# A four-stage attention chain on one core: block transposes on VectorE, kept flags and norm rows as rows, folded copies, a new order

## The chip, the cores and the metric

One core of a Trainium2 chip. The metric is the device time of the whole kernel in microseconds. In the text PE is TensorE, ACT is ScalarE, DVE is VectorE, POOL is GpSimd and SP is SyncE, whose queue issues the DMAs.

## The reference

The input is x and a context, both 128 batches x 128 tokens x 256 channels, f32, and a third array of 64 channels. Four layers run one after the other on every batch:

```python
# L0, 16 heads of 16
mask0 = 1 - all(x == 0, axis=2)
x1 = layernorm(x + mha(x, x, mask0, causal=True))
x2 = layernorm(x1 + mha(x1, context, mask1))     # mask1 from x1
x  = layernorm(x2 + (relu(x2 @ fc1.T + b) * mask0 @ fc2.T + b) * mask0)
# L1, queries x, keys and values norm(context)
nf, nx = norm(x), norm(context)
cross = gelu(attention(nf, nx, nx) @ fc1.T + b) @ fc2.T + b    # width 4 inside
nc = norm(cross)
x = nf + gamma2 * (cross + gamma1 * attention(nc, nc, nc))
# L2
x = x + softmax(x @ context.T) @ context
# L3, 8 heads of 32, then a scan over the 128 tokens
x = x + mha(norm(x), norm(context))
s[t] = silu(s[t-1] @ A.T) + u[t]                 # u from norm(x), 64 states
return x + s @ C + mod
```

In L0, a head's number of valid keys is the count of nonzero energies in its first row, and the masks multiply Q, K, V and the output. The mask on the context's keys and values is the one of x1's tokens.

## The kernel before

**Groups and lags.** Batches go in 64 groups of two. Each engine has a list of steps written out by hand of the form unit.step@lag (PROGRAM, from line 139), and `drive` (line 252) runs 64 + 6 iterations: in iteration i a step with lag l works on group i - l. So at any time groups of seven ages are in work, and a period is one pass through an engine's list. Every step waits on semaphores for what it reads and for its buffer, and engines work strictly in the order of their lists. PSUM has eight banks; which one a step takes is fixed in BANKS. After the 70 iterations all engines meet, and the scan over tokens runs for all 128 batches at once (from line 1582).

**Units.** self_in, self_att, ctx_in, ctx_att and ffn are L0; pair is L1; real is L2; mix_in, mix_att and mix_out are L3. The data of a group stands either "natural" (tokens in partitions; tiles `nat`) or turned (channels in partitions; tiles `trn`, in the profile "turned"), and PE turns the one into the other: a step of four 128x128 transposes against the identity (`turn4`, line 553, line 557 in the profile) into one PSUM bank, which ACT copies out (`evac`, line 903, line 912 in the profile). The steps of this kind that matter here are self_in.xT (x), ctx_in.cT (the context times the flags of x1), real.ccT (the context), and pair.CT (the context normalised, `nat["HC"]`). The context's tile `nat["CC"]` is loaded once more for the last two. A turned x feeds the projections q, k, v (line 565 and 573); the context likewise; the turned normalised context feeds the keys and values of L3 and, scaled by weights (NXT, line 1271), the keys of L1.

**Small work.** POOL multiplies the context by the kept flags (mask, line 1513), copies the flags on so that later groups can overwrite them (lines 1471 to 1484), and adds and scales the norms. The values of L0 leave PSUM by ACT (into VN) and are multiplied by the valid flags on DVE (vp, line 1243). The number of valid keys takes nz, count and spread on DVE, then a matmul by ones (len). The softmaxes of L1 and L2 take a maximum, then a multiplication by minus the scale (nm, line 1288). ACT keeps a copy of x1 for the residual (x1r, line 959).

**The end.** The scan's fresh input and residual lie in DRAM. Its SBUF tile for the input is the upper half of `shared`, where also keys, weights and loaded x tiles of the pipeline live. SP issues the first big piece in iteration 68, inside load_mod of group 62 (scan_early, line 515), after a list of waits for what still uses that memory; it then stores the residual of group 62, behind it in the same queue. res (line 1334), the step of DVE that overwrites the stored tile, waits for that store.

Of the kernel before, what the change touches and what calls it, by code (L numbers as in the profile page):

```python
# [110 lines left out]
def latest(*counts):  # L111

    high = {}
    for c in counts:
# [26 lines left out]
        mix_att.scores.00@6 pair.cross@5 ctx_att.turn.11@4 ctx_att.turn.12@4 ctx_att.values.01@4  # L141
        ctx_att.values.03@4 ctx_att.values.02@4 ctx_att.values.00@4 ctx_att.turn.13@4 ctx_att.turn.10@4
        mix_in.k@5 ctx_att.values.11@4 ctx_att.values.10@4 ctx_att.values.12@4 ctx_att.values.13@4
        ctx_att.back.0@4 real.ccT@5 ctx_in.x1T@3 ctx_att.back.1@4 self_att.scores.00@2 self_att.scores.01@2
        self_att.scores.02@2 mix_att.turn.02@6 ctx_in.cT@3 pair.ncT@5 ctx_in.q@3 pair.sc2@5 mix_att.turn.03@6
        ctx_in.k@3 pair.pT2@5 self_att.scores.11@2 self_att.scores.03@2 self_att.scores.10@2 mix_att.turn.00@6
        pair.av@5 self_in.len@2 self_att.turn.01@2 mix_att.turn.01@6 ffn.x2T@4 mix_att.values.03@6
        mix_att.values.02@6 ctx_in.e0@3 mix_att.values.00@6 mix_att.values.01@6 self_in.xT@1 ffn.fc1@4
        self_att.turn.00@2 self_att.turn.02@2 real.x4T@5 ffn.fc2@4 real.screal@5 mix_out.o@6 self_att.turn.03@2
        real.pTreal@5 self_att.scores.12@2 self_att.scores.13@2 ctx_att.scores.01@3 self_att.values.01@2  # L150
        self_att.values.02@2 self_att.values.00@2 self_att.values.03@2 self_att.turn.11@2 real.av@5 self_in.k@1
        self_in.q@1 self_att.turn.13@2 ctx_in.len@3 self_att.turn.10@2 mix_out.h6T@6 ctx_in.v@3
        self_att.back.0@2 ctx_att.scores.03@3 ctx_att.scores.02@3 ctx_att.scores.11@3 ctx_att.scores.00@3
        self_att.turn.12@2 self_in.v@1 pair.CT@4 self_att.values.13@2 self_att.values.10@2 self_att.values.11@2
        self_att.values.12@2 ctx_att.scores.13@3 ctx_att.scores.12@3 real.h5T@5 ctx_att.turn.01@3 pair.FT@4
        mix_in.v@4 pair.sc1@4 self_att.back.1@2 ctx_att.turn.00@3 mix_in.q@5 ctx_att.turn.02@3 ctx_att.turn.03@3
        pair.pT1@4 self_in.e0@1 pair.av1@4 mix_out.u@6 ctx_att.scores.10@3
    """,
    "act": """
        self_att.probT.13@3 self_att.probT.10@3 self_in.q@2 ctx_in.v@4 pair.lnC@5 pair.lnF@5 self_att.probT.12@3  # L160
        real.ln5@6 self_in.v@2 pair.HCT@5 ctx_att.exp.01@4 self_att.outT.1@3 ctx_att.exp.00@4 ctx_att.exp.03@4
        real.h5T@6 pair.FT@5 ctx_att.probT.01@4 ctx_att.exp.02@4 ctx_att.exp.11@4 mix_in.v@5 ctx_att.probT.00@4
        pair.exp1@5 ctx_att.exp.12@4 mix_in.q@6 ctx_att.probT.02@4 pair.pT1@5 ctx_att.probT.03@4 pair.gelu@5
        self_att.ln1@3 pair.cross@5 ctx_att.exp.13@4 ctx_att.exp.10@4 ctx_att.probT.12@4 mix_att.exp.02@6
        ctx_att.probT.11@4 ctx_att.probT.10@4 ctx_att.probT.13@4 ctx_att.outT.0@4 pair.lnN@5 ctx_att.outT.1@4
# [37 lines left out]
        mix_out.mod@6 ffn.biased@3 self_in.keys@1 self_att.add@2  # L203
# [62 lines left out]
def build(nc, dram):  # L266
# [6 lines left out]
    with ExitStack() as ctx:  # L273
# [25 lines left out]
        for _ in range(16):  # L299
            next(part)  # L300
# [151 lines left out]
        with nc.Block() as block:  # L452
# [637 lines left out]
            def _(dve):  # L1090
                def norm_steps(key, unit, src, ready):
# [3 lines left out]
                    def stats_(g):  # L1095
                        for w in latest(*ready(g)):
                            dve.wait_ge(*w)
# [640 lines left out]
```

## Time and profile before

| | us |
|---|---|
| median of 2 runs | 4029.62 |
| lowest and highest | 4024.6, 4034.65 |
| the profiled execution's own time | 4030.49 |
| its span | 4028.7 |
| PE, ACT, DVE, POOL busy | 3835.5, 3502.7, 3405.5, 2895.3 |

The span is from the first to the last instruction of the profiled execution; its own time is what the device reports for it. Busy times are over the whole span. A number like L557 is a line of the kernel; where a helper records every operation, all its users have that line and are told apart by the names of their tiles.

### The profile page before, as it was taken

How to read it: one execution, taken by the hardware profiler on the slowest of the kernel's cores; microseconds unless marked ns; L12 is line 12 of the kernel's file. 1: busy time of each engine (PE TensorE's matmuls, PEld its weight loads, DVE VectorE, ACT ScalarE, POOL GpSimd, SP SyncE). 2: the span in 40 equal slices, each digit the busy share in tenths (PEclk: the TensorE clock that was granted, in tenths of full speed). 3: DMA queues.
4: the chain of work that ended last, by engine and by line, in shares of the span. 5: the costliest groups of instructions: out<-in, count | busy, mean ns of one | idle time of the engine just before them, and what ended most of it. 6: DMA issues, size and time to landing. Idle time of an engine off the chain costs nothing. (4 is left out here: it accounts for less than half of the span.)

```text
span 4028.7 us, 111616 instructions
## 1 busy us (share of the span) xinstructions
PE 3835.5 (95%) x37177; PEld 3207.8 (80%) x37177; DVE 3405.5 (85%) x9519; ACT 3502.7 (87%) x8460; POOL 2895.3 (72%) x3172
## 2 busy tenths in 40 slices
PE   5999999999999999999999999999999999999859
PEld 3788888888888888888888888888888888888637
DVE  3788988888888898888888898888888898888635
ACT  2899999999999999999999999999999999999735
POOL 1577777777777777777777777777777777777635
PEclk7999999999999999999999999999999999999979
DMA  3001011001101100110111011011101100110038
GB/s 114 20 30 34 19 34 34 26 26 34 34 21 32 34 28 24 34 34 21 32 34 31 21 34 34 23 30 35 34 19 34 34 28 24 34 34 24 16 93 303
DMA packets 121875, 159.92 MB, mean 40 GB/s; under 512 B 12296, under 2 KB 108450, under 8 KB 116642
## 3 DMA queue, kind: packets, MB, share of 16 engines
q1 hardware_dynamic: 116896, 145.39, 11.7%
q8 instruction: 306, 5.01, 0.5%
q10 hardware_dynamic: 4416, 7.41, 0.5%
q14 instruction: 257, 2.11, 0.2%
HBM read 114.86 MB, written 37.75 MB: 38 GB/s over the span
## 5 line engine op out<-in xcount | busy, mean ns | idle before, releaser
L621 PE MATMUL bank<-ident,prob 128*128 128x128 f32 x5120 | 757.1, 280 | 62.6 <-ACT CR L1008 24.5
L941 ACT ACTIVATE probT<-bank 128x512 f32<-128x512 f32 x1280 | 733.4, 596 | 93.9 <-PE bank L621 92.5
L621 PEld LDWEIGHTS bank<-ident,prob 128*128 128x128 f32 x5120 | 572.8, 142 | 233.9 <-issue 138.3
L930 ACT ACTIVATE prob<-prob,mx 128x128 f32<-128x128 f32 x2048 | 646.5, 399 | 23.2 <-DVE mx L1130 23.0
L912 ACT ACTIVATE turned<-bank 128x512 f32<-128x512 f32 x896 | 524.5, 603 | 141.0 <-PE bank L557 109.1
L565 PE MATMUL bank<-turned,shared 128*128 128x256 f32 x2560 | 598.8, 381 | 0.7 <-ACT turned L912 0.7
L1447 POOL TENSOR_TENSOR rs_ln<-ve_ln,half 128x2 f32<-128x2 f32 x320 | 251.2, 785 | 444.8 <-DVE ve_ln L1112 444.8
L1141 DVE TENSOR_REDUCE mx<-bank 128x4 f32<-128x512 f32 x768 | 508.9, 684 | 40.7 <-PE bank L592 38.1
L565 PEld LDWEIGHTS bank<-turned,shared 128*128 128x128 f32 x2560 | 474.0, 191 | 59.0 <-ACT turned L912 1.1
L1152 DVE TENSOR_TENSOR prob<-bank,mx 128x512 f32<-128x512 f32 x768 | 509.5, 677 | 6.7
L922 ACT ACTIVATE prob<-prob 128x512 f32<-128x512 f32 x768 | 461.2, 641 | 10.0 <-DVE prob L1152 9.1
L1526 POOL TENSOR_SCALAR shared<-turned,half_of 128x512 f32<-128x512 f32 x256 | 400.9, 1580 | 87.3 <-ACT turned L912 87.3
L592 PE MATMUL bank<-shared,turned 32*128 32x256 f32 x4096 | 447.5, 403 | 2.3 <-ACT probT L941 1.4
L1123 DVE TENSOR_TENSOR prob<-bank,causal 128x512 f32<-128x512 f32 x512 | 350.3, 684 | 85.7 <-PE bank L621 78.0
L1130 DVE TENSOR_REDUCE mx<-prob 128x4 f32<-128x512 f32 x512 | 348.5, 681 | 22.2 <-ACT prob L930 1.8
L573 PE MATMUL bank<-shared,turned 128*128 128x256 f32 x1536 | 365.4, 381 | 0.4 <-DVE turned L1259 0.2
L592 PEld LDWEIGHTS bank<-shared,turned 32*128 32x128 f32 x4096 | 283.4, 185 | 80.1 <-issue 67.3
L573 PEld LDWEIGHTS bank<-shared,turned 128*128 128x128 f32 x1536 | 278.1, 191 | 31.2 <-DVE turned L1259 1.1
L1461 POOL TENSOR_TENSOR X<-X,row_ln_g 128x512 f32<-128x512 f32 x192 | 244.9, 1276 | 75.3 <-ACT X L991 75.3
L1537 POOL TENSOR_TENSOR prob<-prob,inv 128x512 f32<-128x512 f32 x256 | 266.5, 1042 | 28.8 <-DVE inv L1168 28.7
L655 PE MATMUL bank<-probT,shared 128*32 128x128 f32 x8192 | 277.8, 276 | 0.6 <-ACT probT L941 0.6
L655 PEld LDWEIGHTS bank<-probT,shared 128*32 128x32 f32 x8192 | 208.4, 110 | 65.6 <-issue 43.8
(238 smaller groups left out, 9058.9 us busy)
## 6 DMA issues: line engine op xcount, KB each, us to landing
shared<-in_x SPq DMA_DIRECT2D x128, 256.0 KB, 2.8
CB<-in_ctx SPq DMA_DIRECT2D x64, 256.0 KB, 4.0
CC<-in_ctx SPq DMA_DIRECT2D x64, 256.0 KB, 2.7
mod<-mod_rows SPq DMA_DIRECT2D x64, 256.0 KB, 3.7
residual<-X SPq DMA_DIRECT2D x64, 256.0 KB, 2.2
out<-turned SPq DMA_DIRECT2D x16, 1024.0 KB, 5.0
turned<-residual SPq DMA_DIRECT2D x14, 1024.0 KB, 7.8
u_turned<-us SPq DMA_DIRECT2D x124, 32.0 KB, 1.9
```

Source lines behind the costliest of these rows:

```text
L565: last = nc.tensor.matmul(t[:, m * W:(m + 1) * W], w[:, a, m * 128:(m + 1) * 128], src[:, a, :], start=(a == 0), stop=(a == DH - 1))
L573: last = nc.tensor.matmul(t[:, b * D:(b + 1) * D], src[:, a, b * S:(b + 1) * S], w[:, a, :], start=(a == 0), stop=(a == DH - 1))
L592: last = nc.tensor.matmul(t[:, a * W:(a + 1) * W], QT[p][rows_, a, b * S:(b + 1) * S], KEYS[p][rows_, a, :, b * S:(b + 1) * S], start=True ...
L621: last = nc.tensor.transpose(t[:, h * 128:(h + 1) * 128], src[:, h, :], ident[:])
L655: last = nc.tensor.matmul(t[k * 32:(k + 1) * 32, r * 128:(r + 1) * 128], VP[p][:, b, 4 * r + k, :], src[:, k, :], start=True, stop=True)
L912: nc.scalar.activation(dst, banks.of(f"{unit}.{name}")[:, 0:n], ACT.Copy).then_inc(*st["act"].mark(name))
L922: nc.scalar.activation(flat(t), flat(t), ACT.Exp, scale=SCALE[p]).then_inc(*st["act"].mark(f"exp.{b}{r}"))
L930: last = nc.scalar.activation(t[:, h, :], t[:, h, :], ACT.Exp, bias=low[:, h:h + 1], scale=1.0)
L941: nc.scalar.activation(flat(t), banks.of(f"{att}.turn.{b}{r}")[:, :], ACT.Copy).then_inc(*st["act"].mark(f"probT.{b}{r}"))
L1141: nc.vector.tensor_reduce(m[:], banks.of(f"{att}.tile.{b}{r}")[:, :].rearrange("p (h t) -> p h t", h=4), AX, ALU.max)\
L1152: nc.vector.tensor_tensor(t[:], banks.of(f"{att}.tile.{b}{r}")[:, :].rearrange("p (h t) -> p h t", h=4), maxes.of(f"{att}.max.{b}{r}")[:]. ...
L1526: last = nc.gpsimd.tensor_scalar(KEYS[p][:, :, c, :], KT[p][:], half_of[:, c:c + 1], None, ALU.mult)
```

## The change

1. **x and the context arrive in blocks.** Instead of one DMA per group with rows of 1 KB, four DMAs place blocks of 32 tokens x 32 channels such that one DVE transpose of 128x512 (32x32 blocks) gives the turned tile. self_in.xT moves from PE and ACT to DVE; ctx_in.cT too, now of the unmasked context, into one of three buffers ccT. The plain x is still loaded (XR); its flags are now taken from that.
2. **The kept flags as a row.** ctx_in.kept on PE turns the flags, each broadcast over 128 columns (two transposes), and ctx_in.masked on DVE multiplies ccT by them from PSUM. POOL's mask goes.
3. **real.ccT goes**: real.screal reads the same ccT. The context's plain tile becomes one of three buffers cc in the memory of `shared`; its load moves from lag 3 to lag 2 and waits for real.av three groups back.
4. **Norm rows through DRAM.** lnC's scale and shift (two per token) are stored to DRAM (rowout) and loaded as rows, broadcast to all partitions (rowin). POOL makes the turned normalised context from ccT by a multiplication and an addition (pair.hcs, pair.HCT). lnC and HCT on ACT and CT on PE go; NXT reads SBUF.
5. **Folded.** nz takes its sum along (count goes), spread goes into the len matmul; valid writes its flags straight to where vp needs them; v of both passes leaves PSUM by vp on DVE; the maximum of L1 and L2 is negated in place (nm goes), the scale moves into the weights' scaling or into an evacuation; four copies of flags and x1r go, by more buffers.
6. **New PROGRAM and BANKS** for all engines. The highest lag stays 6.
7. **scan_early waits for more**, because ccT and cc lie where the scan's input goes.

```diff
+    def in_blocks(t, src, g, here):
+        v = t[:].rearrange("p b d -> p (b d)").rearrange("p (a b k i) -> p a b k i", a=DH, b=G, i=32)
+        for j in range(4):
+            sp.dma_start(v[32 * j:32 * j + 32], src[g, j]).then_inc(here.sem, 16)
...
     def load_pair(g):
-        for w in latest(real["pe"].before("av", g)):
+        sp.wait_ge(added, 7)
+        for w in latest(ctx_in3.before(g), real["pe"].before("av", g, 3)):
             sp.wait_ge(*w)
-        sp.dma_start(nat["CC"][:], ctx_g[g]).then_inc(ctx_in3.sem, 16)
+        sp.dma_start(cc[g % 3], ctx_g[g]).then_inc(ctx_in3.sem, 16)
...
     def scan_early():
         n = NG - 1
-        for w in latest(self_in["pe"].done("xT", n), self_in["dve"].done("amax", n), self_in["pool"].done("keys", n),
+        for w in latest(self_in["dve"].done("xT", n), self_in["dve"].done("amax", n), self_in["pool"].done("keys", n),
+                        self_in["pe"].done("v", n), ctx_in["dve"].done("masked", n), pair["pool"].done("HCT", n),
+                        real["pe"].done("screal", n), real["pe"].done("av", n),
...
+    def kept(g):
...
+        for b in range(G):
+            last = nc.tensor.transpose(t[:, b * S:(b + 1) * S], keep1[g % 4][:, b:b + 1].to_broadcast([128, 128]), ident[:])
...
+    def x_turned(g):
+        waits_apart(dve, prep, *latest(x_in.done(g), *(self_in["pe"].before(n, g) for n in "qkv")))
+        nc.vector.transpose(flat(trn["XT"]), x_blocks.rearrange("p b d -> p (b d)")).then_inc(*self_in["dve"].mark("xT"))
...
+    def mask(g):
...
+        nc.vector.tensor_tensor(trn["CBT"][:], ccT[g % 3], t[:, 0:W].unsqueeze(1).to_broadcast([128, DH, W]), ALU.mult)
...
-        nc.vector.tensor_scalar(nz[p][:], banks.of(f"{unit}.e0")[:, 0:S], 0.0, None, ALU.not_equal)
+        nc.vector.tensor_scalar(nz[p][:], banks.of(f"{unit}.e0")[:, 0:S], 0.0, 0.0, ALU.not_equal, ALU.add, accum_out=counts[p][:])
...
+    def hcs(g):
...
+        nc.gpsimd.tensor_tensor(trn["HCT"][:], ccT[g % 3], norm_row[:, 0, :].unsqueeze(1).to_broadcast([128, DH, W]), ALU.mult)
...
     "sp": """
-        self_in.load@0 mix_out.load@6 ctx_in.load@2 mix_out.store@6 self_att.load@2 mix_out.store_u@6
-        pair.load@3
+        mix_out.load@6 pair.rowin@4 pair.load@2 self_in.load@0 ctx_in.load@2 mix_out.store@6 mix_out.store_u@6
+        self_att.load@1 pair.rowout@3
     """
```

In PE's list the context's value steps stood as 01 03 02 00 and, behind two turns and mix_in.k, 11 10 12 13; they now stand as 01 00 02, then 03 12 11, then 13 10, with turns between. real.av is the 64th of the 96 steps of PE's new list (99 before), ctx_in.cT the 13th of the 110 of DVE's.

## Rows read from the trace of the kernel before

In a timeline a row is start (us), length (us), engine, line, operation, tiles and count. In groups a row is busy time in all (us), mean of one (ns), then idle time of the engine before it. By source, durations are least/median/greatest.

**Rows 1.** The page's first part: the span, and each engine's busy time.
```profile
span 4028.7 us, 111616 instructions
...
PE 3835.5 (95%) x37177; PEld 3207.8 (80%) x37177; DVE 3405.5 (85%) x9519; ACT 3502.7 (87%) x8460; POOL 2895.3 (72%) x3172
```

**Rows 2.** Windows, ten periods of the steady part: us, then busy time of each engine.
```profile
1000.00:1585.30 585.30, 574.10 (x5642) 484.11 (x5641) 520.43 (x1461) 536.50 (x1281) 442.20 (x490) 1.00 0.10 30
```

**Rows 3.** The gelu's instructions (line 1001) between 1000 and 3400 us, first and last start.
```profile
L1001 ACT ACTIVATE y5T<-bank,gate_col x82: 359/360/362, 1053.2 to 3394.8; 4x128 f32<-4x128 f32 x82
```

**Rows 4.** Waits from 200 to 3690 us: in total, times, longest (us).
```profile
PE bank L621 <- ACT CR L1008: 23.8, 60, 0.5
...
PE bank L621 <- ACT prob L922: 21.6, 59, 0.4
...
PE bank L761 <- ACT probT L941: 19.3, 55, 0.4
```

**Rows 5.** Timeline of PE in one steady period: start us, us, what.
```profile
1706.03 0.60 PE L557 MATMUL bank<-ident,CC 128*128 128x128 f32 x4
1706.46 0.60 PE L557 MATMUL bank<-ident,X 128*128 128x128 f32 x4
...
1720.16 0.66 PE L557 MATMUL bank<-ident,shared 128*128 128x128 f32 x4
1720.66 1.89 PE L565 MATMUL bank<-turned,shared 128*128 128x256 f32 x8
...
1742.65 0.60 PE L557 MATMUL bank<-ident,HC 128*128 128x128 f32 x4
1743.18 1.08 PE L655 MATMUL bank<-probT,shared 128*32 128x128 f32 x32
1744.19 1.14 PE L592 MATMUL bank<-shared,turned 32*128 32x256 f32 x8
```

**Rows 6.** Groups of instructions, shapes apart: busy us, mean ns, then idle before them.
```profile
L991 ACT ACTIVATE HC<-CC,nmr_lnC,rs_lnC 128x256 f32<-128x256 f32 x128 | 71.3, 623 | 0.8 <-POOL nmr_lnC L1452 0.8
```

**Rows 7.** DVE: groups by line, then two lines that run once, by source.
```profile
L1152 DVE TENSOR_TENSOR prob<-bank,mx 128x512 f32<-128x512 f32 x768 | 509.5, 677 | 6.7
...
L1275 DVE TENSOR_SCALAR turned<-bank,col_n_w,col_n_b 128x256 f32<-128x256 f32 x128 | 63.7, 539 | 8.6 <-ACT turned L968 3.7
...
L1249 DVE COPY shared<-valid_self 128x32 f32<-128x32 f32 x64 | 36.7, 574 | 0.0
...
L1291 DVE TENSOR_SCALAR nmax<-nmx 128x2 f32<-128x2 f32 x128 | 17.7, 138 | 0.1
...
L1360 DVE TENSOR_TENSOR shared<-shared,turned x1: 2283/2283/2283, 46.4 to 46.4; 128x2048 f32<-128x2048 f32 x1
...
L1386 DVE TENSOR_SCALAR w_q<-w_q,col_g x2: 342/343/344, 57.1 to 58.1; 128x256 f32<-128x256 f32 x2
```

**Rows 8.** The page's DMA parts: the main queue, and the residual store.
```profile
q1 hardware_dynamic: 116896, 145.39, 11.7%
...
residual<-X SPq DMA_DIRECT2D x64, 256.0 KB, 2.2
```

**Rows 9.** Timeline of SP's queue near the end of the pipeline.
```profile
3853.28 0.46 SPq L448 DMA_DIRECT2D shared<-u_turned  x1
3853.79 0.86 SPq L450 DMA_DIRECT2D turned<-residual  x2
3889.60 0.41 SPq L509 DMA_DIRECT2D residual<-X  x1
```

**Rows 10.** Windows while the residual chunks load: last columns are clock, DMA share, GB/s.
```profile
3873.00:3913.00 40.00, 21.87 (x138) 16.09 (x138) 13.00 (x35) 11.65 (x24) 11.18 (x13) 0.74 0.17 64
```

**Rows 11.** By source, at the end: real.av; what res (line 1337) waited for; the store's landing.
```profile
L784 PE MATMUL bank<-CC,pct_real x4: 379/379/454, 3883.6 to 3884.3; 128*128 128x256 f32 x4
...
  DMA residual<-X: 7.8, 1
...
DMA to landing us min/median/max: 24.4/24.4/24.4
```

More of the change, by code:

```diff
@@ L140 @@
     "pe": """
[L141 to L155, printed above, removed]
@@ new lines @@
+        pair.rs2@5 self_att.max.00@2 self_att.mask.03@2 pair.sa@5 self_att.max.03@2 self_att.mask.02@2
+        self_att.max.02@2 self_att.mask.10@2 ctx_in.nz@3 self_att.mask.11@2 ffn.relu@4 self_in.vp@2
+        self_att.max.10@2 self_att.max.11@2 self_in.xT@1 ffn.sum@4 ctx_in.valid@3 ffn.ln3stats@4 ffn.ln3aggr@4
+        ffn.ln3ve@4 real.mxreal@5 self_in.amax@2 pair.lnCve@3 mix_out.res@6 real.rsreal@5 mix_out.ln6stats@6
+        self_att.mask.13@2 self_att.mask.12@2 mix_out.ln6aggr@6 self_att.max.13@2 ctx_att.max.01@3
@@ new lines @@
+        self_att.max.12@2 ctx_att.centre.01@3 mix_out.ln6ve@6 real.x5@5 pair.lnFstats@4 pair.lnFaggr@4
+        pair.lnFve@4 real.ln5stats@5 self_in.keep@2 real.ln5aggr@5 real.ln5ve@5 ctx_att.max.00@3
+        self_att.recip.0@2 ctx_att.max.02@3 ctx_att.centre.00@3 self_att.norm.0@2 ctx_att.max.03@3
+        ctx_att.centre.02@3 ctx_att.centre.03@3 ctx_in.vp@3 ctx_att.max.11@3 self_att.recip.1@2 self_in.q0@1
+        pair.NXT@4 self_att.norm.1@2 ctx_att.max.12@3 ctx_att.centre.11@3 pair.mx1@4 ctx_att.centre.12@3
@@ new lines @@
+    mix_in.k:2 ctx_att.out.1:3 ctx_in.x1T:1 ctx_att.back.0:4 mix_att.turn.02:7 ctx_att.back.1:2
+    self_att.tile.00:2 self_att.tile.02:0 self_att.tile.01:6 pair.ncT:4 ctx_in.q:3 pair.sc2:0 mix_att.turn.03:1
+    ctx_in.kept:5 ctx_in.k:3 pair.pT2:1 mix_att.turn.00:4 self_att.tile.10:6 self_att.tile.11:7
+    self_att.tile.03:5 pair.av:1 mix_att.turn.01:2 self_att.turn.01:4 ffn.x2T:3 mix_att.out.0:5 ctx_in.e0:2
+    ffn.fc1:0 self_att.turn.02:4 self_att.turn.00:1 real.x4T:4 ffn.fc2:7 self_in.len:7 self_in.v:3 real.screal:1
@@ new lines @@
+    mix_out.o:7 self_att.turn.03:2 self_att.turn.11:2 real.pTreal:0 ctx_att.tile.01:3 self_att.tile.13:5
+    self_att.tile.12:6 self_att.out.0:4 real.av:0 self_in.k:7 self_att.back.0:0 self_in.q:6 self_att.turn.12:3
+    self_att.turn.10:1 mix_out.h6T:3 self_att.turn.13:7 ctx_att.tile.00:1 ctx_att.tile.03:4 ctx_att.tile.02:5
+    ctx_in.len:0 ctx_in.v:2 self_att.out.1:7 ctx_att.tile.11:6 ctx_att.tile.13:1 ctx_att.tile.12:3 real.h5T:0
+    pair.FT:4 ctx_att.turn.01:5 mix_in.v0:2 mix_in.v1:0 pair.sc1:7 self_att.back.1:7 ctx_att.turn.00:4
@@ L226 @@
+    mix_in.q:5 ctx_att.turn.02:7 ctx_att.turn.03:2 pair.pT1:4 self_in.e0:6 mix_out.u:4 pair.av1:5
 """.split())
```

398 lines of the change are left out of this document (189 added, 209 removed).

## Prediction

> **What bounds the kernel now.** I read the page first. PE is busy for 3835.5 of the 4028.7 us span, ACT for 3502.7 and DVE for 3405.5 [rows 1]; but these are means over a filling, a steady part, a draining and the scan. So I took a stretch of the steady part by windows: in 585.3 us PE is busy 574.1, ACT 536.5, DVE 520.4, POOL 442.2, at a granted clock of 1.00 [rows 2]. The gelu of ScalarE runs once per group of two batches, so its start times give the period: two instructions each, 41 pairs from 1053.2 to 3394.8 us, 2341.6/40 = 58.54 us [rows 3]. Ten periods are that stretch, so per period PE has 57.4 us, ACT 53.7, DVE 52.0 and POOL 44.2. PE is the bound. Of its 1.1 us of idle time nearly all is a wait for ScalarE: 23.8 + 21.6 + 19.3 us in the 59.6 periods from 200 to 3690 us [rows 4]. What counts is therefore what a period costs on PE, times some 61 periods that run at this pace, and then what happens at the ends, which the period does not show.
>
> **PE, per period.** The timeline shows four transposes starting at 1706.03 and the next step at 1706.46: 0.43 us for a group of four (real.ccT; ctx_in.cT has the same 0.43). self_in.xT takes 0.50 until the projection behind it starts and pair.CT 0.53 [rows 5]. All four go: 0.43 + 0.43 + 0.50 + 0.53 = 1.89. ctx_in.kept adds two transposes of the same shape, half a group: 0.22. The new order also splits the eight value steps of the context pass, which now run as two groups of four, in three; one run of four takes 1.01 us to the next start [rows 5], and I put 0.1 for the extra opening and closing (bounds: nothing, and 0.4, another such run less its work). Net 1.57 saved. Scores still come in six runs of different row groups, so they stay.
>
> **ACT.** Nine instructions go, of about 0.62 each: the evacuations of xT, cT, CT, ccT and both v, the X1r copy, and the two halves of the lnC normalisation [rows 6]: 5.5 us, so ACT falls from 53.7 to 48.1. It is under PE now and stays there, so this pays only through the 1.1 us that PE waits for it. I take a third of that back, 0.35; bounds 0 and 1.1. The new period is then 58.54 - 1.57 - 0.35 = 56.6.
>
> **DVE.** Removed: two counts, two spreads and three negations of 0.14 to 0.3, two copies into a stride (0.57 the dearer), and the two NXT halves read SBUF instead of PSUM, 0.54 down to the 0.34 of a scaling of the same size [rows 7]: together 2.7 us of durations, and seven waits of DVE for itself. Added: two block transposes of 128x512, and a masking multiplication from PSUM (the 0.68 of the centring). The trace has no DVE transpose. Nearest row: 0.68, any pass over 128x512. Upper bound: the 2.28 us of a pass over four times as many elements, as if a 4-byte element took four turns [rows 7]; lower bound 0.3, half of the nearest row (a transpose can't give time back). I take 0.7, which gives +2.1 against -2.7, and up to 0.3 for the sum that now rides on the nz comparison: DVE stays at 51.5 to 52, under 56.6, hidden behind PE. At 2.28 each it would be 54.8.
>
> The Trainium skill (VectorE: DVE Perf Modes, The three transpose paths) gives 311 ns for a DVE transpose of 128x128 bf16 in 32x32 blocks and says such a transpose stays inside its blocks, which is why the loads have to place the blocks. Four such would be 1.24 us by an estimate from that page; DVE would have 53 us and the forecast would stand. No run here shows it yet.
>
> **POOL** loses two masking passes and four tiny copies, and gains two passes over 128x512 for the norm of context: about level, 44 of 56.6.
>
> **DMA.** x and one of the context loads become four DMAs each with runs of 32 floats, 2 x 2048 descriptors of 128 bytes per period, 256 per DMA engine. The main queue's 116896 packets took 11.7% of 16 engines' span, 64 ns each at a mean of 1.2 KB [rows 8]; if 128 bytes cost as much, that is 16 us of the 57, and I expect less. The SP queue now puts the context load of a group behind real.av of the same iteration (pair.load waits for it), and behind it come self_in.load and ctx_in.load. real.av is the 64th of PE's 96 steps, and ctx_in.cT the 13th of DVE's 110 in the next iteration, so by their places about (0.33 + 0.12) x 56.6 = 25 us are left for up to 16. The norm rows leave at the end of one iteration and are wanted in the middle of the next. I put nothing.
>
> The skill speaks against this part (DMA: Bandwidth & Descriptors, Specifications): below 512 bytes the engines lose line rate. By that the loads are slow, but it changes the sum only if they exceed the 25 us, which is a rival below.
>
> **The end, where I expect a loss.** At iteration 68 SP issues scan_early: 3.9 MB of fresh scan input at 3853.28 and then two residual chunks at 3853.79 [rows 9]. Those have 122 batches as partitions. The store of residual (62), issued at 3889.60 in the same queue, takes 24.4 us to land, where 2.2 is the median, because it lies behind them, and res(63) on DVE waits 7.8 us for it [rows 8, 9, 11]. While the chunks run, DMA is busy at 0.17 only [rows 10]: about two of the sixteen engines, and the whole takes from 3853.3 to 3914.0, 61 us. The change adds waits to scan_early, because cc and ccT now lie in the scan's memory: real.screal and real.av of group 63. real.av(63) starts its matmuls at 3883.6 and ends about 3884.7 [rows 11]. So scan_early leaves 31 us later, everything behind it too, and res(63), which has no cover left (it is waiting already), goes from 3914.0 to about 3945. The scan follows it by the same steps as now. Price 31 us; bounds 0 (if something else reorders) and 38. Queued behind the waiting SP are the stores of (62), whose landing has its own delay, already counted.
>
> **Sum.** 61 x 1.92 = 117; the three shrinking iterations before the end save about 3 more; the end costs 31: 89 less. The profiled execution's own time is 4030.49 (1.8 us around the span); 4030.5 - 89 = 3941.5, and the median of the two runs is 0.9 below it. I give 3942, 2.2% less. 2% is 81 us, about what a measurement of this kernel can tell from no change.
>
> **Rivals.**
> 1. PE's remaining waits go altogether (ACT relieved by 5.5 us): period 55.9, 4030.5 - 61 x 2.64 - 3 + 31 = 3898. For it: nearly all PE idle is ScalarE's. Against it: DVE is now the second bound, at 92%. Chance 0.13.
> 2. The end doesn't lengthen: 3911. Against it stand the added waits. Chance 0.10.
> 3. The waits stay or new ones come, because evacuation moved from ACT (idle 4.9 us) to DVE, whose work doesn't shrink while the period does: period 57.0 to 58.2, 3965 to 4038, middle 3990. Chance 0.24.
> 4. The other side: the block transposes are slow and DVE becomes the bound. At 2.28 us each DVE has 54.8 us of work, and it now stands idle for 6.5 us a period; if 5 of these stay as latency the period is 59.8 and the time 4030.5 + 61 x 1.26 + 31 = 4138. It decides from about 1.6 us per transpose (53.5 + 5 = 58.5). Chance 0.05.
> 5. The changed loads don't arrive in the 25 us: each us that cT is late is a us of period; only above 64 ns x 1.5 per packet. Or the loads aren't split as written. 4060 to 4100. Chance 0.03.
> The forecast case has the remaining 0.45, with 3915 to 3972 as its own span.
>
> **How the numbers follow.** Faster by over 2% (below 3949): 0.27 of the forecast case, all of 1 and 2: 0.50, and 0.02 of 3: 0.52. Slower by over 2% (above 4110): half of 4 and 5 with a little of unknown kinds: 0.05. The rest, 0.43, within 2%. Range 3893 to 4022: it leaves out 4 and 5, the upper end of 3 and the lower of 1.
>
> **What would show it.** Right: gelu starts 56.6 us apart; PE about 55.8 busy per period, ACT 48, DVE about 52; four-transpose groups of X (shared), CB, CC and HC gone; a DVE transpose near 0.7 us; the scan input issued right after real.av(63), and res(63) waiting some 39 us for the residual's DMA. Wrong: a period over 57.2 with PE idle, DVE above 54, long waits of DVE transposes for DMA, or scan input that leaves before real.av(63).

## The result and the profile after

The changed kernel takes 3986.64 us (median of two runs, 3986.45 and 3986.82) against 4029.62: a ratio of 0.9893, 95% interval 0.9877 to 0.9909. It is 1.1% faster. I had forecast 2.2%, 3942 us, so about half of the forecast gain came, and the time stands inside my range and in the band of my third rival.

The first lines of the page, which answer to [rows 1] and [rows 8]:

```profile
span 3985.0 us, 108660 instructions
...
PE 3772.9 (95%) x36281; PEld 3090.5 (78%) x36281; DVE 3380.8 (85%) x9264; ACT 3267.6 (82%) x7884; POOL 2860.4 (72%) x2916
...
DMA packets 401412, 176.68 MB, mean 44 GB/s; under 512 B 316425, under 2 KB 379811, under 8 KB 396195
...
q1 hardware_dynamic: 396448, 162.33, 18.5%
```

PE has lost 62.6 us, ACT 235, and the main queue moves 3.4 times as many packets.

The steady part first. The gelus, now line 1012, answer to [rows 3]:

```profile
L1012 ACT ACTIVATE y5T<-bank,gate_col x84: 357/358/361, 1041.5 to 3391.6; 4x128 f32<-4x128 f32 x84
```

41 periods in 2350.1 us: 57.32 us each, where I had said 56.6. But they are not alike. Windows over three single periods, to be laid beside [rows 2] (us, busy time of PE, PEld, DVE, ACT, POOL, granted clock, DMA share, GB/s):

```profile
1442.29:1499.35 57.06, 56.44 (x552) 46.59 (x551) 51.57 (x143) 50.03 (x120) 43.73 (x46) 1.00 0.16 36
1499.35:1556.40 57.05, 56.43 (x552) 46.51 (x551) 51.35 (x143) 50.03 (x120) 43.49 (x45) 1.00 0.16 35
2070.94:2131.90 60.96, 58.02 (x556) 47.86 (x552) 51.89 (x144) 50.14 (x120) 44.09 (x48) 0.97 0.22 33
```

The undisturbed period is 57.05 us. The third took 60.96 with the same work. Of the 57 periods from the fourth gelu to the 61st, 13 are more than 0.3 us above the median, and all 57 together are 17.6 us above it; in the kernel before the same sum was 1.0 us. How much it is differs from execution to execution: two kernels below with the same stores (blocks_plain, tail_split) have 31.3 and 33.2 us in their profiles. Where the span changed, by the gelus' starts (us):

```
                         before    after   difference
start to 4th gelu         350.7    350.3     -0.4
4th to 61st (57 periods) 3336.5   3269.6    -66.9   (-83.4 by the median period, +16.6 irregular, rest rounding)
61st to 64th              164.2    159.4     -4.8
64th to first scan step    75.8    104.4    +28.6
scan                      101.5    101.3     -0.2
```

The end was as expected. SP's timeline (start, length), to be compared with [rows 9], and under it, by source, what res (L1342) waited for, beside [rows 11]:

```profile
3810.16 0.48 SPq L449 DMA_DIRECT2D shared<-u_turned  x1
3810.69 0.86 SPq L451 DMA_DIRECT2D turned<-residual  x2
3814.98 29.88 SPq L527 DMA_DIRECT2D residual<-X  x1
3844.90 7.09 SPq L559 DMA_DIRECT2D shared<-us  x2
...
  DMA residual<-X: 38.7, 1
```

The store of residual (62) needs 29.9 us only to be issued, and res(63) stands 38.7 us (I had said some 39).

Groups of DVE and POOL (busy us, mean ns, then idle before them):

```profile
L1261 DVE TENSOR_TENSOR shared<-bank,shared 128x512 f32<-128x512 f32 x128 | 87.8, 686 | 59.2 <-PE bank L593 59.2
...
L1203 DVE STREAM_TRANSPOSE turned<-shared 128x512 f32<-128x512 f32 x64 | 44.9, 701 | 4.7 <-DMA shared<-in_x 4.7
L1209 DVE STREAM_TRANSPOSE shared<-CB 128x512 f32<-128x512 f32 x64 | 44.8, 700 | 0.0
...
L1509 POOL TENSOR_TENSOR turned<-shared 128x512 f32<-128x512 f32 x64 | 83.6, 1306 | 0.0
```

The block transposes take 0.70 us as estimated. The block loads keep them waiting 4.7 us in the whole run, all of it at one time.

### The profile page after: what moved, and what is told of

The parts are those of the page before. It is cut to its first block and busy times, and to the rows that moved or that the text cites. A ratio compares the mean times of both kernels' runs of the same rounds, so it can differ in the third digit from the quotient of the medians.

```text
span 3985.0 us, 108660 instructions
## 1 busy us (share of the span) xinstructions
PE 3772.9 (95%) x36281; PEld 3090.5 (78%) x36281; DVE 3380.8 (85%) x9264; ACT 3267.6 (82%) x7884; POOL 2860.4 (72%) x2916
## 5 line engine op out<-in xcount | busy, mean ns | idle before, releaser
L641 PE MATMUL bank<-ident,prob 128*128 128x128 f32 x5120 | 767.9, 279 | 13.5 <-DVE mx L1147 5.3
L641 PEld LDWEIGHTS bank<-ident,prob 128*128 128x128 f32 x5120 | 585.2, 142 | 162.4 <-issue 97.5
L585 PE MATMUL bank<-turned,shared 128*128 128x256 f32 x2560 | 617.0, 384 | 19.8 <-DVE turned L1203 19.5
L932 ACT ACTIVATE turned<-bank 128x512 f32<-128x512 f32 x704 | 410.3, 592 | 198.5 <-PE bank L577 179.1
L942 ACT ACTIVATE prob<-prob 128x512 f32<-128x512 f32 x768 | 471.9, 631 | 6.4 <-DVE prob L1158 5.4
L1453 POOL TENSOR_TENSOR rs_ln<-ve_ln,half 128x2 f32<-128x2 f32 x320 | 223.9, 700 | 333.5 <-DVE ve_ln L1118 333.5
L675 PE MATMUL bank<-probT,shared 128*32 128x128 f32 x8192 | 316.0, 278 | 32.7 <-ACT probT L961 25.2
L1129 DVE TENSOR_TENSOR prob<-bank,causal 128x512 f32<-128x512 f32 x512 | 341.3, 677 | 2.9 <-PE bank L612 2.0
L675 PEld LDWEIGHTS bank<-probT,shared 128*32 128x32 f32 x8192 | 198.3, 109 | 139.7 <-issue 77.1
L1468 POOL TENSOR_TENSOR X<-X,row_ln_g 128x512 f32<-128x512 f32 x160 | 204.0, 1275 | 96.8 <-ACT X L1002 94.9
```

Source lines behind the costliest of these rows:

```text
L585: last = nc.tensor.matmul(t[:, m * W:(m + 1) * W], w[:, a, m * 128:(m + 1) * 128], src[:, a, :], start=(a == 0), stop=(a == DH - 1))
L641: last = nc.tensor.transpose(t[:, h * 128:(h + 1) * 128], src[:, h, :], ident[:])
L675: last = nc.tensor.matmul(t[k * 32:(k + 1) * 32, r * 128:(r + 1) * 128], VP[p][:, b, 4 * r + k, :], src[:, k, :], start=True, stop=True)
L932: nc.scalar.activation(dst, banks.of(f"{unit}.{name}")[:, 0:n], ACT.Copy, scale=scale).then_inc(*st["act"].mark(name))
L942: nc.scalar.activation(flat(t), flat(t), ACT.Exp, scale=SCALE[p]).then_inc(*st["act"].mark(f"exp.{b}{r}"))
```

## What an irregular period looks like

ACT's timeline in the period that took 60.96 (in brackets the idle time before, and what ended it), then PE's:

```profile
2079.73 0.65 ACT L942 ACTIVATE prob<-prob 128x512 f32<-128x512 f32 x1
2082.81 0.60 ACT L976 ACTIVATE outT<-bank 128x512 f32<-128x512 f32 x1 [2.43 <-remote]
2083.30 0.59 ACT L932 ACTIVATE turned<-bank 128x512 f32<-128x512 f32 x1
...
2087.91 1.08 ACT L932 ACTIVATE turned<-bank 128x512 f32<-128x512 f32 x2 [3.01 <-PE bank L577]
```

```profile
2079.42 0.43 PE L675 MATMUL bank<-probT,shared 128*32 128x128 f32 x8 [0.29 <-ACT probT L961]
...
2080.71 0.38 PE L768 MATMUL bank<-ident,keep 128*128 128x128 f32 x2
2083.55 1.08 PE L688 MATMUL bank<-ident,outT 128*128 128x128 f32 x4 [2.46 <-ACT outT L976]
2084.43 2.94 PE L585 MATMUL bank<-turned,shared 128*128 128x256 f32 x8
```

ACT stops for 2.43 us and the profile finds no releaser in the core ("remote"). What it waits to copy has long been computed (PE's value steps, L675, end at 2079.85), and DVE and POOL stand too. PE follows 0.7 us later. It then pays a second time. The window behind the stop:

```profile
2084.00:2088.00 4.00, 4.00 (x17) 3.26 (x18) 3.20 (x8) 0.99 (x3) 2.56 (x3) 0.68 0.65 116
```

The granted clock is 0.68 in the mean, between full (2.4 GHz) and half (1.2 GHz), after PE has stood for 2.46 us, and a projection that takes 1.89 [rows 5] takes 2.94.

My first suspicion was that the engines lacked their next instruction. The trace has the instruction fetches as DMA packets of 16 and 8 KB. From 400 to 3500 us, durations in ns:

```
                16 KB: number, median, longest, over 2 us    8 KB: number, median, longest, over 1 us
before                 246     1093     1514     0                 208      444      969     0
after                  246     1057     4098    21                 207      474     3005    14
```

By their place in the period, the slow ones start 3 to 15 us after a gelu. The 128-byte block loads run 40 to 50 us after it; the 512 four-byte stores of the norm rows run 2 to 5 us after it. That made theory A (the stores) and theory B (the block loads).

Both take slow fetches for what stops the engines, and the same trace doesn't bear that part out. From the 4th to the 61st gelu 38 fetches are slow by this measure; 34 of them start in periods of even length, which stay at 57.05 in the median. Nine of the 13 long periods have none, the longest among them, and the one shown above has one of 1.39 us that starts at 2085.66, after the stop. What does go with the long periods is another sign, in the trace's record of semaphore updates. PE's signal that ACT's copy waits for is recorded at 2082.72, 2.9 us after the matmuls' end, and those of three more steps of PE, ended between 2080.44 and 2081.09, follow within 0.16 us. Counted over the 57 periods, with a signal of PE called late when it is recorded more than 0.5 us after the end (PE's ends are modelled; in the median it is 0.015):

```
                long periods, with a late    with a slow   slow fetches in all,
                              signal of PE   fetch         in even periods
after                     13            12             4          38     34
blocks_plain              19            19             4          34     30
tail_split                20            17             9          36     27
before_stores             46            45            37          55      9
packed_stores             54            54            23          30      1
norm_packed                1             0             0           5      5
packed_loads               1             0             0           3      3
before                     0             0             0           0      0
```

The other kernels of this document, all without the small stores, have no late signal either. In the changed kernel the late signals come 9.2 to 11.9 us after a gelu, and the last of the 4-byte stores lands 8.4 to 12.1 us after it, as far as that is recorded. Why a store should hold up a signal no run shows. In the kernels with these stores a part of the updates is missing from the record (21340 recorded in the changed kernel, 21664 in norm_packed), so signals of other engines may be late too.

## Experiments: the irregular periods

**norm_small.** The edit:

```diff
-    sp.dma_start(norm_d[k].rearrange("(b s o) -> s b o", b=G, o=1), t[:].unsqueeze(2), ...)
+    sp.dma_start(norm_d[k].rearrange("(b s o) -> s b o", b=G, o=1)[0:1], t[0:1, :].unsqueeze(2), ...)
...
-    sp.dma_start(norm_row, norm_d.partition_broadcast(128))
+    sp.dma_start(norm_row, x_d[0, 0:2, :].partition_broadcast(128))
```

> The changed kernel, but only the first token's scale and shift of the context's norm are stored (4 numbers of 4 bytes each period in place of 512), and the row that POOL multiplies and adds is read from x: the norm of the context in L1 and L3 is left out so far. In the changed kernel 13 of the 57 steady periods are over 0.3 us longer than the shortest, 17.6 us above the median in sum, and instruction fetches that start 6 to 9 us after a gelu take 3.1 us (16 KB) where the median elsewhere is 1.05. Theory A, the 4-byte stores slow the instruction fetches and so stop the engines: the sum above the median falls below 3 us, no fetch takes over 1.6 us, and the time is about 16 us less, 3970. Theory B, the 128-byte runs of the block loads do it: nothing changes, 3987. Theory C, it is the wait of SP or POOL for the row: 3970 as well, but the fetches stay slow.

Measured: 3963.93 us, ratio 0.9832 [0.9814, 0.9849]. The sum above the median is 1.1 us, and no 16 KB fetch takes over 1.84 us, no 8 KB one over 0.75. The period stays at 57.05. Theory A by both its signs, as far as it names the stores, and no signal of PE is late. Theory C is excluded by before_stores below, where nobody waits for the stores.

**blocks_plain.** Each of the four DMAs now reads `x_g[g, 32*j : 32*j+32]` into the same 32 partitions, in place of `x_q[g, j]`; so for the context.

> The changed kernel, but x and the context are loaded in runs of 1 KB (four DMAs of 32 partitions each) where it places blocks of 128 bytes: the turned tiles then hold the wrong elements, so L0's first projections and the context's keys are of other data. Theory B, the 128-byte runs cause the irregular periods: their sum above the median falls from 17.6 us to under 3 and the time is 16 us less, 3970. Theory A, the 4-byte stores: unchanged, 13 or so long periods, 3987 give or take 4. If DMA traffic as such cost PE or DVE anything, the median period of 57.05 would fall too; I expect it to stay within 0.03.

Measured: 3981.94 us, 0.9874 [0.9857, 0.9892]; in the profile 19 long periods, 31.3 us above the median, 19 fetches over 2 us (this execution is the longest of four, which took 3977.3 to 3991.0). Theory B falls. The median period is 57.07: 4096 runs of 128 bytes a period cost nothing in the steady part.

**norm_packed.** The edit:

```diff
+    norm_four = sb("norm_four", [128, 2 * G])        # rs_lnC | nmr_lnC
...
-    for k, t in enumerate((rs["lnC"], nmr["lnC"])): sp.dma_start(norm_d[k]..., ...)
+    sp.dma_start(norm_d, norm_four[:])               # norm_d is (S, 2 * G)
...
+    norm_of = norm_row.rearrange("p (s k b) -> p k b s", k=2, b=G)   # POOL reads this
```

> The changed kernel with scale and shift in one tile of four columns, stored by one DMA of 128 runs of 16 bytes in place of two of 256 runs of 4, and read by POOL with a stride of four numbers. Nothing is left out. Theory A (small stores slow the fetches, in proportion to their count): a quarter of the excess stays, under 5 of 17.6 us, so 3974. If the strided read costs POOL more, its two passes of about 1.0 us grow; POOL has 13 us of idle time a period, so the time doesn't show it. Theory B: 3987.

Measured: 3961.40 us, 0.9828 [0.981, 0.9845]; 1.2 us above the median, not the quarter that I allowed. Two 16 KB fetches still take 2.9 and 4.1 us, in periods that are not long. The edit changes the number of runs, their size and the number of DMAs together; which of them counts no run tells. Its gain over the changed kernel by the profiles' marks: 5.8 us up to the 4th gelu, 16.7 in the 57 periods, 2.0 and 0.6 behind. POOL pays for the stride and nobody waits for it (groups of norm_packed; 1.31 in the changed kernel):

```profile
L1512 POOL TENSOR_TENSOR turned<-shared 128x512 f32<-128x512 f32 x64 | 99.3, 1552 | 0.0
```

What was left: are such stores enough by themselves, and is it their number or their direction? Three kernels with added DMAs that nobody reads:

```diff
 def store_u(g):
     ...
+    for w in latest(dummy_out.before(g)):
+        sp.wait_ge(*w)
+    for k in range(n):       # stores: n = 2 or 4, 256 elements each; loads: the same with the two sides exchanged
+        sp.dma_start(dummy_d[k].rearrange("(b s o) -> s b o", b=G, o=1), ident[:, 2*k:2*k+2].unsqueeze(2), ...)
```

**before_stores**

> The kernel before, with two more DMAs a period on SP's queue, each storing 256 numbers of 4 bytes (from the identity, to a DRAM tensor that nobody reads). Nothing is left out. Its periods are even now: 1.0 us above the median in sum over 57. Theory, four-byte stores by themselves slow the instruction fetches and stop the engines: 10 to 30 us above the median in sum, fetches of 3 us, time 4040 to 4060. Rival, they hurt only a kernel that waits for them (SP waits for the rows in the changed kernel): under 3 us in sum, 4030 to 4033.

Measured: 4151.67 us, ratio 1.0301 [1.0284, 1.0318]: 3% slower, far above what I allowed. I had measured the damage against the median; here most periods are hit, so the floor is the better base. The shortest period is still 58.51, the mean 60.35: 1.84 us x 57 = 105 us. Two neighbouring periods by windows, one spared and one hit:

```profile
1440.53:1499.04 58.51, 57.39 (x569) 48.42 (x568) 53.03 (x146) 53.59 (x128) 44.15 (x50) 1.00 0.11 30
1499.04:1561.62 62.58, 59.70 (x566) 49.83 (x564) 51.98 (x146) 53.82 (x129) 44.18 (x50) 0.97 0.11 28
```

ACT's waits there show the same sign as in the changed kernel (in total, times, longest):

```profile
ACT outT L964 <- remote: 25.2, 12, 2.4
```

**packed_stores** and **packed_loads**

> packed_split with 1024 four-byte stores a period in four more DMAs, twice what the changed kernel had. Nothing is left out. If the damage goes with the number: 35 to 60 us above the median in sum over the 57 periods (1.2 in packed_split), time 3970 to 4000. If only a fetch that happens to fall into the window is hit: some 18 to 30 us.

> packed_split with 1024 four-byte loads a period, from x to a spare tile. Nothing is left out. If it is the number of small descriptors, the same as packed_stores; if it is the stores to DRAM, whose completion is slow (the 512 of the changed kernel take 6.4 us until SP sees them landed), then under 5 us above the median in sum, time within 6 us of packed_split's 3934.8. I hold the second for likelier, since 4096 runs of 128 bytes a period do nothing.

Measured: 4138.59 us (1.0268 [1.0251, 1.0285]) with 1024 stores, periods of 57.06 to 62.81, mean 60.33: 186 us above the floor. For that damage it has 15 fetches of 16 KB over 2 us, where the changed kernel has 21 for its 18 us: once more the fetches don't measure it. With 1024 loads of 4 bytes 3938.99 us (0.9776 [0.976, 0.9792]), 1.0 us above the median, no fetch over 1.8 us and no late signal. So it is small stores to DRAM, not small descriptors. The damage is not simply in proportion: 512 stores cost 18 us in the changed kernel and 105 in the kernel before, where they run 0 to 2 us after the gelu in place of 2 to 5, beside other fetches. That this place decides is argued only: no run moved the same stores alone.

## Experiments: the end

**tail_split.** The edit, and the count that the scan waits for raised by one:

```diff
     for k in chunks:
-        sp.dma_start(res_t[k][b, :, :], res_d[b, k * TC:(k + 1) * TC, :]).then_inc(res_in[k], 16)
+        for part in (slice(0, 112), slice(112, EARLY)):
+            sp.dma_start(res_t[k][part, :, :], res_d[part, k * TC:(k + 1) * TC, :]).then_inc(res_in[k], 16)
```

> The changed kernel, but the first two residual chunks of the scan (122 batches as partitions, which move at 52 GB/s, 244 packets of 8 KB from 3832 to 3869 us, while the scan's input before them moves at 200 GB/s) are loaded as 112 and 10 partitions each. My theory is that the partition count spreads over two DMA engines only, and that res(63) waits for the store of residual (62) behind them: with 112 on sixteen engines the two chunks take 10 us in place of 38, plus some 3 for the 10 partitions, res(63) starts about 25 us earlier and the time is 25 us less, 3962 (bounds 3955 and 3970). Rival: the chunks are slow by their DRAM pattern (8 KB of every 128 KB), whatever the count: 3987.

Measured: 3962.97 us, 0.9827 [0.9809, 0.9844]; from the last gelu to the scan 75.9 us in place of 104.4. That is 28.5 us; the median fell by 23.7, since the small stores are still there and cost more in its profiled execution (33.2 us against 17.6). That my 25 fits is in part luck. res(63) waits 10.0 us, by source:

```profile
  DMA residual<-X: 10.0, 1
```

The partition count is the cause. The Trainium skill (DMA: Bandwidth & Descriptors, Why a DMA increments its semaphore by 16 and not by 1) says that a DMA uses the largest number of engines up to 16 that divides the slowest dimension of both its sides: two for 122, sixteen for 112. The trace of the changed kernel agrees, by windows while the scan's input moves (64 partitions) and while the chunks do (last columns: clock, DMA share, GB/s):

```profile
3815.00:3820.00 5.00, 4.08 (x11) 3.20 (x12) 0.00 (x0) 0.60 (x1) 1.27 (x1) 0.50 0.98 200
3835.00:3840.00 5.00, 4.07 (x31) 3.08 (x24) 0.00 (x0) 0.60 (x1) 0.00 (x0) 0.50 0.13 52
```

0.13 of sixteen engines is two.

**before_split.** The same edit on the kernel before.

> The kernel before with the first two residual chunks as 112 and 10 partitions. Its own res(63) waits only 7.8 us for the store of residual (62). Theory, that wait goes: 4030 - 8 = 4022, and the time from the last gelu to the scan falls from 75.8 to 68. Rival, the scan's first steps then wait for something else that came at the same time: within 3 us of 4030.

Measured: 4030.18 us, 1.0003 [0.9994, 1.0013]. The rival. res(63) no longer waits for the store, but 6.9 us for PE, where it waited 7.8. The slow chunks cost the kernel before nothing that can be measured; only behind the later start do they cost 28.5 us.

**packed_split** and **packed_later.** Both corrections together, and in the second `if g == NG - 2: scan_early()` made `NG - 1`.

> Both corrections together on the changed kernel: the norm numbers in one store of 16-byte runs, and the residual chunks as 112 and 10 partitions. If the two are independent (one acts in the steady part, one at the end), their gains add up: 3986.6 - 25.2 (norm_packed) - 28.5 (the time from the last gelu to the scan in tail_split against the changed kernel) = 3933, period mean 57.07, 76 us from the last gelu to the scan. If the end only took over what the norm had cost there, some 3945.

> As packed_split, but the scan's big input is issued one iteration later, after the modulation load of group 63, so that neither the store of residual (62) nor that load lies behind it. Theory: the 20 us in which the scan's input fills all engines no longer lie ahead of res(63), and the rest of what the end costs goes: up to 8 us less than packed_split, 3925 to 3933. Rival: the scan's input then is itself what the scan waits for, 5 to 15 us more than packed_split, 3938 to 3948.

Measured: packed_split 3934.79 us, 0.9767 [0.9753, 0.978]; packed_later 3940.56, 0.9779 [0.9766, 0.9793]. The gains add up as expected, and packed_split beats both kernels: 2.3% faster than before. Its gelus and one stretch of five periods by windows:

```profile
L1013 ACT ACTIVATE y5T<-bank,gate_col x84: 357/358/362, 1030.8 to 3370.9; 4x128 f32<-4x128 f32 x84
```

```profile
1601.36:1886.60 285.24, 282.15 (x2752) 232.86 (x2751) 257.81 (x711) 250.06 (x596) 221.37 (x226) 1.00 0.16 35
```

57.08 us a gelu, 57.05 in the stretch. packed_later took its rival's way. The scan's input is issued at 3801.45 in place of 3784.64 and now lies ahead of the last group's own transfers: the last residual store, issued at 3824.36, lands 9.7 us later, where packed_split's, issued at 3821.83, takes 2.2.

## Experiments: what PE and ACT are worth

**before_no_turns.** In the kernel before, for xT, cT, ccT and CT:

```diff
-    turn4(t, src)                                            # four of 128x128
+    nc.tensor.transpose(t[:, 0:32], src[0:32, 0, 0:128], ident[0:32, 0:32])
```

> The kernel before, with the four groups of transposes (x, context, context again, normalised context) cut to one transpose of 32x128 each, whose 32 columns ACT and DVE read sixteen and eight times over, so that their work keeps its size; the turned x, context and normed context are left out by that. PE has 1.9 us a period in these groups, and some 0.4 of it stays. Theory of the prediction, PE's time pays in full: period 58.52 - 1.5 = 57.0, time 4030 - 92 = 3938. Rival, ACT (53.6 busy) and DVE are so close that half comes back as waits: period 57.8, 3985.

Measured: 3991.54 us, 0.9909 [0.9894, 0.9924], period 57.81: 0.71 less, not 1.5. That is my rival's number, but not for its reason: no wait came back. Five periods by windows:

```profile
1626.95:1916.03 289.08, 283.76 (x2764) 235.39 (x2763) 258.50 (x730) 267.37 (x640) 223.12 (x246) 1.00 0.10 30
```

PE's idle time is (289.08 - 283.76)/5 = 1.06 a period, where it was 1.13. The missing part is PE's own. By start-to-start times the four groups fell from 1.90 to 0.69, and four other steps rose by 0.09 to 0.10 each (self_in.v 1.73 to 1.82, ffn.fc1 1.73 to 1.83, mix_att.turn.02, ctx_att.back.0), two by 0.06. The stub's cheapness was my error: it uses 32 of 128 rows, as scores do, and I take it (no run changed that alone) that the step before such a tile costs more. The changed kernel has two untouched steps that fit: mix_out.o (1.73, then 1.82) and mix_out.h6T (0.44, then 0.53) have a score or a value step behind them only there. So my allowance of 0.4 for the stub should have been 1.2. The run supports that PE's time pays fully, and shows that a step's price hangs on its neighbour.

**act_more.** packed_split and nine copies on ACT:

```diff
     nc.scalar.activation(dst, banks.of(...), ACT.Copy, scale=scale).then_inc(...)
+    if f"{unit}.{name}" in spare:      # nine of the evacuations
+        nc.scalar.activation(spare[...], ident[:].unsqueeze(1).to_broadcast([128, 4, 128]), ACT.Copy)
```

> packed_split plus nine copies of 128x512 on ACT from the identity to spare tiles, one behind each of nine evacuations: nothing is left out. ACT goes back from 50.0 us a period to about 55.5, somewhat over the 53.6 that it had before the change. The prediction gave ACT's relief 0.35 us a period: then this is 0.35 x 61 = 21 us slower than packed_split, 3954. Rival a, ACT's load is worth nothing while PE has 56.4: the same as packed_split within 4 us. Rival b, each copy delays the step behind it by 0.6 us and PE waits for several of them: 1 to 2 us a period, 60 to 120 us slower.

Measured: 3996.40 us, 0.9916 [0.9901, 0.9931], period 58.03 (windows):

```profile
1628.35:1918.53 290.18, 285.42 (x2752) 232.09 (x2751) 257.81 (x711) 270.52 (x640) 221.65 (x226) 1.00 0.15 35
```

ACT has 54.1 in place of 50.0 and the period is 0.98 longer: 60 us in all, nearly three times the 21 that my step gives, and not nothing, as my rival a had it. It is the low end of my rival b: start to start, the 0.98 is spread over PE's transposes of the probabilities (0.38), the value steps of L3 (0.20) and four other kinds of step. ACT is no bound here, but it stands between PE's steps. The price is that of these nine places, not of ACT's load as such.

**values_run, values_late, scores_swap.** Three orders of PE's list on packed_split; the first is

```diff
-    ctx_att.turn.13 ctx_att.values.03 .12 .11 ctx_att.turn.10 self_in.len ctx_in.x1T ctx_att.values.13 .10
+    ctx_att.turn.13 ctx_att.turn.10 self_in.len ctx_in.x1T ctx_att.values.03 .12 .11 .13 .10
```

the second has turn.10, len and x1T ahead of the second run and mix_att.turn.02 ahead of the third, and the third exchanges the last two steps of the list.

> packed_split with one change in PE's list: the eight value steps of the context pass stand in two runs (three, then five) in place of three; ctx_att.turn.10, self_in.len and ctx_in.x1T move ahead of the second run. By the steps' start-to-start times, the three runs cost 3.06 us a period in the changed kernel (2.46 before the change), of which 0.77 are waits for ACT's probT. Theory, the split of the run is a term that the prediction mis-sized (0.1 given, about 0.27 measured, plus the waits): the period falls by 0.2 (opening and closing) to 0.9 (the waits too), 12 to 55 us less than packed_split, 3880 to 3923. Rival, other steps take the waits over (outT and back.0 come later): no change within 6 us.

> packed_split with the second and third run of context values each moved some 1 us later in PE's list (turn.10, len and x1T ahead of the second, turn.02 of L3 ahead of the third). The three runs stay; only the waits for ACT's probT (0.77 us a period) can go. Theory, these waits are real losses: period down by 0.3 to 0.7, 18 to 43 us less than packed_split. Rival, PE waits for the same ACT steps at the next place: no change within 6 us.

> packed_split with ctx_att.scores.10 ahead of mix_att.scores.00 in PE's list, as in the kernel before. In the changed kernel the step scores.10 takes 1.16 us to the next start, before it 0.81. Theory, this 0.35 is a cost of the new neighbour (a step of other shape behind it) and goes: 21 us less than packed_split, 3914. Rival, its bank (the one of mix_out.u) isn't free in time, since DVE takes u as the last step of its list: PE waits some 0.5 us more, 30 us slower, 3965.

Measured: 3957.71, 3967.74 and 3980.54 us (0.9821 [0.9805, 0.9838], 0.9846 [0.9829, 0.9862], 0.9882 [0.9866, 0.9899]): all slower than packed_split, against the theory of each; only scores_swap's rival had the sign (30 us slower expected, 46 measured). In values_run the value steps did fall by 0.77, and ctx_att.turn.13 and turn.10 together rose by 1.11, because turn.10 now stands where its exp isn't done; values_late has the same 1.11, and its value steps, in three runs and without a wait, take 2.16. In scores_swap PE waits for DVE to take u out of the bank (PE's waits, first of values_run, then of scores_swap):

```profile
PE bank L642 <- ACT prob L943: 44.9, 42, 1.1
```

```profile
PE bank L613 <- DVE us L1349: 26.7, 41, 1.0
```

The short waits in the changed order are the cheap ones. I could not better it.

## Why the prediction was right and wrong

**Right:** the end. I gave 31 us for the later scan_early; it is 28.6, with res(63) waiting 38.7 (SP issues it 30.9 us after the last gelu, 1.9 before the change). Right too: 0.70 for the block transposes (not the 1.24 that the prediction estimates beside it), DVE at 51.4 to 51.6, the block loads hidden, POOL level, PE the bound. Two slips that change nothing: 3941.5 less 0.9 is 3940.6, not 3942, and the measurement tells a difference of 0.2% from none, not only one of 2%.

The period fell by 1.466, where I gave 1.92. I take it apart by start-to-start times in the undisturbed periods (ns, medians). "Without waits" is what the same steps take where nothing holds them up; the line of the untouched steps is what the others leave:

```
                                              before   after   change   given
the four groups of transposes                   1896       0    -1896   -1890
ctx_in.kept                                        0     302     +302    +220
8 value steps of the context, without waits     2024    2161     +137    +100
16 score steps, without waits                   6227    6256      +29       0
untouched steps beside other neighbours                          +292       0
waits for ACT                                   1577    1247     -330    -350
period                                         58518   57052    -1466   -1920
```

**Wrong, first step: "PE, per period ... Net 1.57 saved".** PE's own steps gave 1.14, 0.43 less. I priced the steps that go and come (0.14 of the error: kept 0.08, the split of the value steps 0.04, the scores 0.03) and put all others at nothing, and that is the larger part: 0.29 for steps that only stand beside other ones, as mix_out.o and mix_out.h6T with 0.09 each. before_no_turns has the same kind of rise; that the neighbour is its cause is an inference from the two, which no run changed alone. "Scores ... stay" holds for the price of the steps.

**The second step, "ACT ... I take a third of that back, 0.35", has the right size by luck.** ACT fell by 3.6, not 5.5: it has 50.0, not 48.1, partly because an instruction of 0.6 overlaps the next: in the timeline above two of them start at 2082.81 and 2083.30. I took a part of the old waits to go. All three went or shrank, those of [rows 4] (by start-to-start times they are 1.58 us, not the 1.1 of the idle time, for a matmul's record runs on over part of a wait), and new ones came: 0.90 at the value steps for probT, and 0.35 at ctx_att.scores.10. That step takes 1.16 us to the next start, 0.81 before, because the step behind it, pair.cross, needs the gelu. Timelines of the changed kernel (PE, then ACT) and of the kernel before:

```profile
1499.06 1.02 PE L612 MATMUL bank<-shared,turned 32*128 32x256 f32 x4
1500.22 0.48 PE L801 MATMUL bank<-w_cross,y5T 32*128 32x256 f32 x2
...
1499.35 0.73 ACT L1012 ACTIVATE y5T<-bank,gate_col 4x128 f32<-4x128 f32 x2
```

```profile
1461.93 1.13 PE L592 MATMUL bank<-shared,turned 32*128 32x256 f32 x4
1462.74 1.20 PE L608 MATMUL bank<-keys,turned 32*128 32x128 f32 x32
1463.74 0.64 PE L773 MATMUL bank<-w_cross,y5T 32*128 32x256 f32 x4
...
1462.79 0.73 ACT L1001 ACTIVATE y5T<-bank,gate_col 4x128 f32<-4x128 f32 x2
```

In the changed kernel pair.cross starts 0.144 to 0.146 us after the gelu's end in every undisturbed period. Before, mix_att.scores.00 (L608) stood between and covered the wait. In scores_swap, which puts it back there, pair.cross starts 0.43 us after the gelu's end and waits for it no more; the bank then costs more than that gave. So the old waits were paid back with new ones by the new order of PE's list, which I had priced at 0.1.

Both steps together: 0.45 x 57 = 26 us.

**Wrong, third step: "The norm rows leave at the end of one iteration and are wanted in the middle of the next. I put nothing".** As a transfer they were in time. As 512 stores of 4 bytes they stop the engines now and then: 16.6 us in the steady part and 25 in the whole run (norm_packed), about as much as the first two steps together. With the 26 that is more than the 45 that are missing; the end and the last iterations gave some 4 back. That the stores are the cause is shown, by taking them away and by adding them elsewhere; how they do it is open. The trace shows late signals of PE in nearly every long period, and slow fetches mostly in even ones. I asked of every DMA only when it lands, and looked at the wrong one: the many packets of 128 bytes are harmless.

The Trainium skill (Runtime: NRT & Kernel Launch, Instruction fetch mechanics) says that each engine fetches its instructions in 16 KiB blocks by a DMA queue of its own while it executes, and that this is mostly hidden. The 16 KB packets in the trace agree with the blocks, and even of the slow fetches of the changed kernel 34 of 38 start in periods of even length.

My third rival (waits that stay or new ones from the shift between ACT and DVE, period 57.0 to 58.2, middle 3990) has the right number, 57.32, and half the reason: new waits of PE came, but for ACT. DVE's work is where it was, and no new wait of PE for DVE came.

## What to carry to other kernels

Store small per-token numbers in the longest runs that the tile gives, and let the reader take the stride: 128 runs of 16 bytes cost nothing here, 512 of 4 bytes cost 18 to 105 us. When all engines stop together and the profile names no releaser, look for small stores that land at that time, and count any sign that you suspect in the even periods too: the slow fetches were there all along. Give a DMA that others queue behind a partition count that divides by 16. And price a changed order of TensorE steps by start-to-start times with their neighbours, not by the steps that go, and ask of each step whether what it waits for is now covered by the one ahead of it.

## What the runs showed of the hardware beyond what I expected

- With 512 stores of 4 bytes to DRAM a period, signals of finished PE steps are recorded late, up to 2.3 us after the last step that gives them (3.7 in before_stores), and engines stop for 2 to 3 us; instruction fetches are slow 35 times (16 KB over 2 us, 8 KB over 1 us) from 400 to 3500 us, where norm_packed has 5. With 1024 loads of 4 bytes, or 4096 runs of 128 bytes, no signal is late.
- After PE stood for 2.46 us the granted clock was 0.68 over 4 us, a further 1.05 us on one projection.
- A DMA of 122 partitions moves at 52 GB/s and holds up the issue of the next one in its queue by 29.9 us.
- Nine copies on ACT, each behind an evacuation, cost PE 0.24 us per us of work at a load of 50 to 54 of 57.
